# Graph attention on one core: adjacency in 2 MB loads, and packing two tiles ahead of the pick

## What is computed

```python
h = relu(layernorm(x))
support = h @ weight                                   # per head
scores = leaky_relu(f1[m] + f2[n], 0.2)                # f1 = support.u, f2 = support.v
masked = scores * adj                                  # adj: 8192 x 8192 int32, about 4 ones a row
attn = softmax over the nonzero entries of masked
out = x + attn @ support + bias + h @ proj_w.T + proj_b
```

## Time and profile before

| | before |
|---|---|
| median of 3 runs | 870.88 us (867.28 to 871.4) |
| the profiled execution | 878.59 us, span 876.8 us |
| PE / DVE / POOL / ACT busy | 80 / 73 / 60 / 14 % |
| DMA | 329.82 MB, 376 GB/s over the span |
| mean granted TensorE clock | 0.91 |

### The profile page before, as it was taken

One profiled execution on the slowest core, in us unless ns is written; L12 is line 12 of the kernel. 1 busy time (PEld: TensorE's weight loads), 2 busy tenths in 40 slices (PEclk: granted clock), 3 DMA queues, 4 the chain that ended last, 5 costly groups with the idle time before them and its releaser, 6 DMA issues.

```text
span 876.8 us, 11157 instructions
## 1 busy us (share of the span) xinstructions
PE 699.3 (80%) x3011; PEld 429.8 (49%) x3011; DVE 640.9 (73%) x2740; ACT 126.7 (14%) x467; POOL 526.5 (60%) x598
## 2 busy tenths in 40 slices
PE   2989999999855878878777687887778787787665
PEld 0656666666423544444544345554444454444354
DVE  4566665666525887979788797887879788799474
ACT  0223333333210101000010100000100010100000
POOL 4445555445375676676666666666676767666530
PEclk9999999999956999989999988989999899999868
DMA  8999999999997999999999999999999999999930
GB/s 317 420 414 417 418 410 421 420 417 412 424 402 263 362 402 379 383 409 383 401 381 387 392 379 403 375 402 380 372 404 380 403 384 403 381 383 408 409 108 34
DMA packets 63855, 329.82 MB, mean 376 GB/s; under 512 B 12795, under 2 KB 15560, under 8 KB 31024
## 3 DMA queue, kind: packets, MB, share of 16 engines
q1 hardware_dynamic: 43056, 286.28, 81.3%
q0 software_dynamic: 18432, 34.30, 10.8%
q10 hardware_dynamic: 2304, 8.52, 2.4%
HBM read 328.99 MB, written 16.91 MB: 394 GB/s over the span
## 4 chain that ended last, share of the span: by engine, by line
PE 40%; DVE 18%; issue 18%; DMA 16%; another core or an unknown queue 4%; POOL 2%; ACT 1%; SPq 1%; POOLq 0%; ACTq 0%
DMA adj_raw<-in_adj 13%; PE ps_words L400 11%; PE ps_agg L461 8%; PE ps_agg L381 6%; PE ps_two L381 6%; PE ps_two L400 3%; DVE att L930 3%; DVE cand L784 2%; DVE base L940 2%; PE ps_words L392 1%; DMA att<-in_x 1%; SPq L317 1%; PE ps_score L445 1%; DVE codes_rest L809 1%
## 5 line engine op out<-in xcount | busy, mean ns | idle before, releaser
L714 POOL DMA_INDIRECT att<-support_table,idx x384 | 412.6, 1074 | 205.9 <-issue 107.3
L461 PE MATMUL ps_agg<-att,ident 128*128 128x260 f32 x640 | 183.4, 442 | 41.8 <-DVE att L930 41.7
L400 PE MATMUL ps_words<-adj_raw,pack_w 128*128 128x512 fp8e4 x640 | 177.9, 415 | 13.8 <-DMA adj_raw<-in_adj 13.7
L461 PEld LDWEIGHTS ps_agg<-att,ident 128*128 128x128 f32 x640 | 136.6, 220 | 76.0 <-issue 51.5
L400 PEld LDWEIGHTS ps_words<-adj_raw,pack_w 128*128 128x128 bf16 x640 | 61.1, 104 | 107.5 <-issue 32.3
L400 PE MATMUL ps_two<-adj_raw,pack_w 128*128 128x512 fp8e4 x384 | 104.4, 418 | 8.8 <-DMA adj_raw<-in_adj 8.3
L930 DVE TENSOR_TENSOR att<-att 128x1536 f32<-128x1536 f32 x64 | 109.4, 1751 | 0.4 <-ACT att L622 0.4
L784 DVE MAX8 cand<-ps_words 128x8 f32<-128x128 f32 x320 | 67.2, 284 | 47.5 <-PE ps_words L400 47.5
L705 POOL COPY record<-att 128x8 f32<-128x8 f32 x64 | 14.3, 223 | 113.2 <-ACT att L566 113.2
L400 PEld LDWEIGHTS ps_two<-adj_raw,pack_w 128*128 128x128 bf16 x384 | 36.9, 106 | 67.4 <-issue 21.1
L381 PE MATMUL ps_agg<-w_all,hT 128*128 128x260 f32 x256 | 63.0, 389 | 4.1 <-ACT hT L562 4.1
(11 more groups left out here) (118 smaller groups left out, 773.3 us busy)
## 6 DMA issues: line engine op xcount, KB each, us to landing
adj_raw<-in_adj SPq DMA_DIRECT2D x256, 1024.0 KB
support_table<-att ACTq DMA_DIRECT2D x16, 520.0 KB, 8.4
att<-in_x SPq DMA_DIRECT2D x16, 512.0 KB, 7.5
out<-base SPq DMA_DIRECT2D x15, 512.0 KB
att<-support_table,idx POOLq DMA_INDIRECT x384
out<-base SPq DMA_DIRECT2D x4, 128.0 KB
w_all<-in_proj_wT SPq DMA_DIRECT2D x2, 128.0 KB, 5.6
w_all<-in_weight SPq DMA_DIRECT2D x2, 128.0 KB, 6.0
```

Source lines behind the costliest of these rows:

```text
L400: mm = nc.tensor.matmul(ps_words[buffer_of(t)][:, k * 512:(k + 1) * 512], pack_w[:, u * UT + s, :], adj_low[:, n % HELD, s, k * 512:(k + 1 ...
L461: mm = nc.tensor.matmul(ps_agg[:, b, 0:ROW], ident[:] if k < OWN else onehotT[:, g % RING, b], gathered[:, g % RING, b, k], start=(k == 0) ...
L714: pool.indirect_dma_start(gathered[:, g % RING, b, k, :], None, table, bass.IndirectOffsetOnAxis(idx[:, g % RING, b, k:k + 1], 0), bounds_ ...
```

## The change

- UNITS 4 to 2 and HELD 6 to 4: adjacency loads of 2 MB, 8 MB held in place of 6 MB. A load is 8 matmuls of packing. To make room, `spare`, `uv_row`, `projb_row`, `place_hi` and `hT` become views of tensors that are not yet in use.
- Before the second stage PE packs tile 17 whole, and in turn g it packs `t + 2` for each `t` that is picked in that turn. The PSUM areas stay two.
- In turn 30 the last tile is packed load by load between other steps, with `aggregate(28, 1)` ahead of `edge_refs(29)`; in turn 31 `aggregate(29, 1)` goes ahead of `edge_refs(30)`.
- On DVE, `output(28, 1)` goes ahead of the last pick, `output(29, 1)` ahead of `weigh(30)`, and `weigh(31)` ahead of `output(30, 1)`.

```diff
-UNITS = 4
-HELD = 6
+UNITS = 2
+HELD = 4
...
-                    if q > 0:
-                        pack_unit(g + 1, q - 1)
+                    if q > 0 and q % (LOAD // UNITS) == 0:
+                        pack_unit(g + 1, q // (LOAD // UNITS) - 1)
...
             pe.wait_ge(s_staged, TILES)
+            pack_places(FIRST + 1)
+            for u in range(UNITS):
+                pack_unit(FIRST + 1, u)
             for g in range(LATE):
-                new = [t + 1 for t in picks[g]]
+                new = [t + 2 for t in picks[g] if t + 2 < TILES - 1]
                 offsets(g)
                 pack_places(new[0])
                 for u in range(UNITS // 2):
...
             offsets(LATE)
+            pack_places(TILES - 1)
+            for u in range(UNITS // 2):
+                pack_unit(TILES - 1, u)
             aggregate(LATE - 2, 0)
             edge_records(LATE)
             row_scores(LATE - 1)
+            aggregate(LATE - 2, 1)
+            for u in range(UNITS // 2, UNITS - 1):
+                pack_unit(TILES - 1, u)
             edge_refs(LATE - 1)
-            pack_places(TILES - 1)
-            for u in range(UNITS):
-                pack_unit(TILES - 1, u)
-            aggregate(LATE - 2, 1)
+            pack_unit(TILES - 1, UNITS - 1)
...
             row_scores(LATE)
+            aggregate(LATE - 1, 1)
             edge_refs(LATE)
-            aggregate(LATE - 1, 1)
...
             shift(LATE - 1)
+            output(LATE - 2, 1)
             picked = split_words(TILES - 1, 1, pick_words(TILES - 1, 0))
             list_own(LATE + 1, 1, 1)
-            output(LATE - 2, 1)
             weigh(LATE - 1)
...
             shift(LATE)
+            output(LATE - 1, 1)
             weigh(LATE)
-            output(LATE - 1, 1)
...
             shift(LATE + 1)
+            weigh(LATE + 1)
             output(LATE, 1)
-            weigh(LATE + 1)
```

More of the change, by code:

```diff
@@ L95, in gat_kernel @@
         spilled = sb("spilled", [P, TILES], BF16)
-        spare = sb("spare", [P, 4, HF])
         WIDE = RING * GS * BLOCKS * ROW
@@ L107, in gat_kernel @@
         assert 2 * XN + SN <= WIDE
-        uv_tmp = spare[:].rearrange("p (q c) d -> p q c d", q=2)
+        uv_tmp = base[:, TILES - 4:].rearrange("p (q c) d -> p q c d", q=2)
+        uv_row = base[:, TILES - 6:TILES - 4]
+        projb_row = base[:, TILES - 7]
+        place_hi = base[0:2, TILES - 9:TILES - 7].rearrange("p a d -> p (a d)").bitcast(BF16)
         ident = sb("ident", [P, P])
@@ L115, in gat_kernel @@
         w_all = sb("w_all", [P, KC, 2, ROW])
-        uv_row = sb("uv_row", [P, 2, HF])
         bias_row = sb("bias_row", [P, HF])
-        projb_row = sb("projb_row", [P, HF])
         eps_col = sb("eps_col", [P, 1])
@@ L122, in gat_kernel @@
         place = sb("place", [2, WORDS], BF16)
-        place_hi = sb("place_hi", [2, WORDS], BF16)
         bit_mask = sb("bit_mask", [P, BITS], I32)
@@ L131, in gat_kernel @@
         row_no = sb("row_no", [P, P])
-        hT = sb("hT", [P, 2, KC * P])
         stats = sb("stats", [P, LOAD, 6])
@@ L153, in gat_kernel @@
         onehot = sb("onehot", [P, 2, GS, P])
+        hT = onehot[:].rearrange("p a b m -> p a (b m)")
         onehotT = sb("onehotT", [P, RING, GS, P])
@@ L276, in gat_kernel @@
             att[:, P + q * H * P:P + (q + 1) * H * P].rearrange("p (h m) -> p h m", h=H) for q in range(5))
-        dn_out, dn_x, dn_xhat, dn_base = (spare[:, q, :] for q in range(4))
+        dn_out, dn_x, dn_xhat, dn_base = (base[:, q, :] for q in range(4))
         dn_rest = att[:, P + 5 * H * P:]
@@ L323, in _ @@
                              (bias_row[:, :], bias),
-                             (projb_row[:, :], proj_b.rearrange("(o d) -> o d", o=1))):
+                             (projb_row, proj_b.rearrange("(o d) -> o d", o=1))):
                 sp.dma_start(dst, src.to_broadcast([P, HF])).then_inc(s_w_in, 16)
@@ L694, in _ @@
             pool.wait_ge(s_w_in, 16 * W_LOADS)
-            const(pool.tensor_tensor(bias_row[:], bias_row[:], projb_row[:], ALU.add))
+            const(pool.tensor_tensor(bias_row[:], bias_row[:], projb_row, ALU.add))
             assert const.n == POOL_CONSTS
```

## The result

| | before | after |
|---|---|---|
| median | 870.59 us (867.28 to 871.4) | 966.79 us (965.12 to 969.57) |
| ratio, 95% interval | 1 | 1.1108 (1.108 to 1.1137) |
| profiled execution | 878.59 us, span 876.8 | 969.57 us, span 967.8 |
| granted TensorE clock | 0.91 | 0.868 |
| one turn of the second stage | 19.00 us | 22.37 us |

The change makes the kernel 11% slower. The forecast of 973 us holds. Of the reasons under it, one (loads of 2 MB cost nothing) falls with the experiments, and another (DVE sets the pace of the old loop) is put in doubt by them. An execution that stands more than 1.5% above the fastest of its kernel is left out of the ratios; this befell one execution, of `small_first` (904.56 us).

The account below looks back on a forecast made before the run. DVE with its PE hand-overs was taken as the bound, DMA only nearly full. 113.7 for the loop + 2 at the start - 13.5 at the end = +102 us on the 870.9 us median: 973 us, range 905 to 1015 us.

Parts of the forecast that it names:

- loads of 2 MB cost nothing: Adjacency loads: larger ones taken at 0, covered by DVE's turn; bounds -15 us and +2 us at the start.
- DVE sets the pace of the old loop: Second stage: DVE and its hand-overs with PE pace the turns at 19.0 us; DMA is only nearly full.
- The added wait: DVE at `list_spill`: waits 3.5 us a turn for copied records, plus 1.7 for the clock; 5.2 us, 145.6 over 28 turns.
- Rival 2: PE's clock costs nothing after its longer gap: +54.6 us, 926 us; chance 0.18.
- What takes some of it back: Turns with one pick: DVE's old 31.9 us of waiting before L936 absorbs added delay, leaving +113.7 us.
- so I go by DVE: Second stage: DVE has no wait descending from adjacency loads, so DVE is taken as pace although the chain names loads.
- rival 1: Second stage: DMA is the bound and the change frees it, records copied by T + 4.2; 842 us; chance 0.10.
- if DMA stays full: Sign in the second stage after: DMA share not clearly under 1.00 would mean the loads had been the bound.
- Rival 3: Hand-over of `aggregate(g-2, 1)` moves along with the delay, so DVE's 31.9 us of waiting stay: +134, 1005 us; chance 0.17.
- Packing tile 17 first: Before turn 2: sixteen matmuls (3.6 us) ahead of `offsets(0)`, taken at +2 us, bounds -5 and +6.
- The last turns: Turns written by hand: new order of packing, outputs and weighing gives -13.5 us, bounds -18 and 0.
- The term of -8.5: Last pick: its 10.56 us wait shrinks by packing earlier, aggregation puts 2.74 on `shift(29)`; net -8.5 us.

Follow-up runs that it names:

- small_first: The kernel before with tile t + 2 packed and tile 17 first, PE doing all small steps ahead of all packing; 890.1 us, ratio 1.023.
- warm_again: The changed kernel plus 28 useless matmuls a turn in PE's idle time before the places, second run; 902.39 us, ratio 1.038.
- before_again: The kernel before, unchanged, run for a second profile; 882.36 us, one run.
- tail_only: The kernel before with only the last two turns of the changed one; 865.07 us, ratio 0.993.
- loads_split: The kernel before with 2 MB buffers, four held, each filled by two DMAs of 1 MB; 875.8 us, ratio 0.9959.
- loads_only: The kernel before with only the loads changed, 2 MB each and four held; 937.31 us, ratio 1.076.
- the slower set: Set 2 of the three sets of runs, each with its own runs of the unchanged kernel before; that kernel's median there is 880.15 us.
- ahead_only: The kernel before with PE packing tile t + 2 and tile 17 first, 1 MB loads and old last turns; 968.82 us, ratio 1.1124.
- warm: The changed kernel plus 28 useless matmuls a turn in PE's idle time before the places, first run, in set 2; 957.69 us, ratio 1.0893.

## Why the prediction was right, and where it was not

**The added wait: right.** It took 3.5 us a turn at full clock and 1.7 us for the clock. Filled gaps leave 86.7 / 28 = 3.1 us, and the clock costs (152.1 - 86.7) / 28 = 2.3 us. Together 5.4 us a turn (5.6 in after, 155.7 / 28) against 5.2; the one part was foretold 0.4 us too large and the other 0.6 us too small. The place (`list_spill`), the mechanism (steps behind a waiting `pack_places`) and PE's idle time before the places are those foretold. Rival 2 (the clock costs nothing) falls with warm_again. The added sizes lie within the bounds given, 0 to 3.4 us for the clock.

**What takes some of it back: the right place, the wrong size.** The step "in the turns with one pick DVE had to wait anyway before L936, 31.9 us in all" failed in size: 155.7 us were added and the loop grew by 94.4, so that 61.3 us were taken back, 2.2 us a turn in the mean. The place was right for the most part: the 13 turns with one pick grew only from 18.7 to 20.3 us in the mean, which gives back some 52 us, and the 15 with two from 19.3 to 24.2, which gives back some 9. What was short is the count: L936 is one row of 13 in the list of DVE's waits from 277 to 809 us, which add up to 62.5 us; beside the new wait, after has only 4.6 us of waits left. The likely reason lies in an earlier step, "so I go by DVE". The turn of before is 18.9 to 19.1 us in before, before_again, tail_only and loads_split, that is wherever t + 1 is packed with packets of 8 KB, although DVE waits for different things in them; DMA is at a share of 0.99 to 1.00 in all four, at 388 to 392 GB/s from 350 to 750 us, and in tail_only PE waits 47 us for adjacency. This points to the loads as the pace of the old loop. The engines could have done a turn in some 22.4 - 5.6 = 16.8 us, had the data come; the 2.2 us up to 19.0 were slack that the added wait used up first. Single turns bear this out: in loads_only and tail_only turns with one pick took as little as 14.7 us, against 18.7 in before. If so, rival 1 was right about the bound and wrong about what the change does to it. The sign that the prediction names for it, "if DMA stays full", could not show it: a loop made slower leaves DMA unfilled, whatever paced it before. No run took DMA work out of the old loop, so this is inferred from equal turns and not shown by itself. The page's slices and the chain of waits had both named the loads; a list of waits in which no row says "DMA" was no proof against them, since DVE waits for PE and PE for the data. The same trace shows the second link, in PE's waits from 277 to 809 us:

```profile
PE ps_words L400 <- DMA adj_raw<-in_adj: 10.3, 7, 2.2
...
PE ps_two L400 <- DMA adj_raw<-in_adj: 7.2, 6, 1.8
```

That is 17.5 us here and 47 in tail_only, at the same turn, so the size of this wait does not measure the bound either.

**Rival 3** (the late hand-over moves along) had nothing to move: no wait stands before `denom` in after, and in the old loop it came only with the slower set.

**Loads of 2 MB: wrong, and hidden.** "Larger ones have next to nothing to give" was true. That they could take something was bounded at +2 us, and alone they cost 66. The bound looked only at the adjacency and at PE, not at the other user of the same DMA engines. It did no harm to the sum because the other wait covers it.

**Packing tile 17 first**: +6.6 us against +2, just beyond the bound of +6. ahead_only starts turn 2 at 276.1 us, loads_only at 284.5 and tail_only at 270.2, so both the extra packing and the large loads are in it. Before's own 277.0 is from a profile that looks like set 2; tail_only, the same code up to there, starts turn 2 at 270.2, and against it the changed kernel is 13.4 us late.

**The last turns**: -10.0 against -13.5 between the two profiles, within the bounds, but -5.7 us in the medians of tail_only. The term of -8.5 in the forecast is also more than its own parts give (-10.56 + 2.74 = -7.8). The wait of 10.56 us before the last pick is 0.5 us now; in its place DVE waits 2.5 us for the records of turn 30 and 3.5 us for the references, and part of the 10.56 us went with the slower set: with the old last turns this wait is 6.6 us in loads_only and 7.2 in ahead_only, but 9.5 in before_again.

**The sum** gave +102, and the spans differ by 91.0. 29.4 us more were taken back than counted (61.3 against 31.9), and 18.2 us more were added than counted (10.1 by the wait, 4.6 before turn 2, 3.5 at the end). These errors cancelled for the most part, so it is partly luck that the forecast of 973 us lies so near to 966.79; the medians differ by 96.2.

## What to carry to other kernels

Before a step that waits is put into an engine's queue, list what stands behind it and who waits for that: here a buffer taken one tile too early held up three small steps that another engine needs each turn, and the mended order gave back four fifths of the loss. Where small DMAs share the engines with a stream, keep the stream's packets small; a larger load may have nothing to give and much to take. And costs that fall on the same place in a turn do not add up: undo them together, or the second one comes out from under the first.

## What was not expected of the hardware

- Loads of 2 MB (packets of 16 KB) in the adjacency stream raise the median time to landing of a gather from 6.3 us (tail_only) to 8.1 (loads_only), the longest from 7.7 to 14.4, and DVE's waiting for them in the loop from 2.1 to 97.3 us. Filling the same buffers by two DMAs each, with the same bytes in flight, removes the waiting.
- 28 useless matmuls a turn (4.71 us) made the kernel 63.5 us faster, since PE came out of its wait at the higher clock.
- The same kernel, warm, took 957.69 us in one set and 902.39 us in another, while before differed by 12 us only (880.15 and 868.52). In the slower set DVE waits for PE's results with no releaser that the profile names. That a kernel in which a hand-over from PE sets the pace suffers more from it is suggested by this one pair and not shown. Sets 1 and 2 ran on the same chip, so the chip is not what tells them apart; why the sets differ stays open.
